# A state-space scan and an FP4 feed-forward on one core: D term as a matmul, ScalarE copies the sum out, TensorE's sums behind its other jobs

## The reference, cut to what matters

```python
x = silu(conv(x) + conv_b); xh = x.reshape(b, L, 4, 128)
dt_r, Bm, Cm = split(einsum('hod,blhd->blho', xw, xh))
delta = softplus(einsum('hdr,blhr->blhd', dtw, dt_r) + dt_b)
def step(s, inp):
    s = s * exp(d_t * A) + (d_t * u_t) * B_t
    y_t = einsum('bhdn,bhn->bhd', s, C_t)
...
y = ys + x * Dskip          # the D term
y = y * silu(z)
x = x + y @ out_proj_w.T
x = x + fp4_ffn(layernorm(x))
```

## Time and profile before

| | |
|---|---|
| median of three runs | 4897.47 us |
| the profiled execution | 4895.54 us |
| its span, first to last instruction | 4893.5 us |
| TensorE, matmul records / weight loads | 4234.6 us (87%) / 1986.9 us (41%) |
| VectorE | 4549.8 us (93%) |
| ScalarE | 3509.2 us (72%) |
| GpSimd | 3429.2 us (70%) |
| mean granted clock of TensorE | 0.988 of full speed |

### The profile page before, as it was taken

One profiled execution on the slowest core, in us unless ns is written; L12 is line 12 of the kernel. 1 busy time (PEld: TensorE's weight loads), 2 busy tenths in 40 slices (PEclk: granted clock), 3 DMA queues, 4 the chain that ended last, 5 costly groups with the idle time before them and its releaser, 6 DMA issues. The chain is left out here.

```text
span 4893.5 us, 64416 instructions
## 1 busy us (share of the span) xinstructions
PE 4234.6 (87%) x18927; PEld 1986.9 (41%) x19244; DVE 4549.8 (93%) x6828; ACT 3509.2 (72%) x5783; POOL 3429.2 (70%) x2321
## 2 busy tenths in 40 slices
PE   4788888888888888888898888888888888888887
PEld 1234444444444444444444444444444444444434
DVE  6999999999999999999999999999999999999994
ACT  3777777677777777777777777777777777777763
POOL 4777777777776777777777677777777677677763
PEclk8999999999999999999999999999999999999999
DMA  2333333333333333333333333333333333333330
GB/s 89 140 135 123 127 129 125 121 132 126 120 133 124 123 129 129 123 123 134 119 127 131 122 126 127 127 123 130 126 120 133 124 123 129 129 123 123 129 117 19
DMA packets 211138, 600.59 MB, mean 123 GB/s; under 512 B 25446, under 2 KB 76774, under 8 KB 210790
## 3 DMA queue, kind: packets, MB, share of 16 engines
q1 hardware_dynamic: 209088, 594.30, 35.6%
q10 hardware_dynamic: 1702, 2.16, 0.2%
HBM read 575.39 MB, written 20.97 MB: 122 GB/s over the span
## 5 line engine op out<-in xcount | busy, mean ns | idle before, releaser
L629 POOL TENSOR_TENSOR prod<-state,cs 128x1024 f32<-128x1024 f32 x1024 | 2416.5, 2360 | 1320.8 <-DVE state L852 1295.2
L440 ACT ACTIVATE decay<-delta,aneg 128x512 f32<-128x512 f32 x2048 | 1432.6, 717 | 925.3 <-DVE state L852 916.7
L840 DVE TENSOR_TENSOR db<-db,du 128x512 f32<-128x512 f32 x2048 | 1392.0, 680 | 56.7 <-PE db L904 55.5
L852 DVE TENSOR_TENSOR_SCAN state<-decay,carry,db 128x512 f32<-128x512 f32 x1024 | 1292.4, 1262 | 0.0
L852 DVE TENSOR_TENSOR_SCAN state<-decay,db 128x512 f32<-128x512 f32 x1024 | 1232.6, 1204 | 0.0
L904 PE MATMUL db<-pieces,sel 128*128 128x512 bf16 x1798 | 690.1, 386 | 393.5 <-DVE state L852 384.6
L919 PE MATMUL ybank<-prod,ident 64*64 64x512 f32 x4096 | 1003.4, 608 | 28.0 <-DVE hh L790 27.0
L919 PE MATMUL cross<-prod,ident 64*64 64x512 f32 x4096 | 1003.1, 609 | 0.0
L904 PEld LDWEIGHTS db<-pieces,sel 128*128 128x128 bf16 x2048 | 197.8, 97 | 1039.9 <-DVE state L852 809.0
L919 PEld LDWEIGHTS ybank<-prod,ident 64*64 64x64 f32 x4096 | 255.8, 134 | 455.1 <-issue 417.8
L1040 PE MATMUL bank_a<-wd,ht 128*128 128x256 f32 x1536 | 406.0, 389 | 3.2 <-DVE state L852 2.0
(11 more groups left out here) (124 smaller groups left out, 6399.6 us busy)
## 6 DMA issues: line engine op xcount, KB each, us to landing
cs<-c_rows SPq DMA_DIRECT2D x1024, 512.0 KB, 3.6
xin<-in_hidden SPq DMA_DIRECT2D x128, 128.0 KB, 3.6
xres<-in_hidden SPq DMA_DIRECT2D x128, 128.0 KB, 3.4
out_x<-ot SPq DMA_DIRECT2D x128, 128.0 KB, 3.6
c_rows<-xdbl SPq DMA_DIRECT2D x128, 32.0 KB, 3.6
win<-in_win_t SPq DMA_DIRECT2D x1, 1024.0 KB, 10.6
state<-in_w_gate ACTq DMA_DIRECT2D x1, 704.0 KB
state<-in_w_up ACTq DMA_DIRECT2D x1, 704.0 KB
```

The source lines that it names most:

```text
L440: act.activation(decay[:, g.val() % RING, :], delta[:, gu % 2, :], ACT.Exp, scale=aneg[:, gu % HEADS, gn:gn + 1]).then_inc(decayed, 1)
L629: pool.tensor_tensor(prod[:, r, :, :], state[:, 2 * p:2 * p + 2, :], cs[:, c, :, :], ALU.mult).then_inc(weighted, 1)
L840: dve.tensor_tensor(t[:, :], t[:, :], du[:, gu % 2, :], ALU.mult).then_inc(db_done, 1)
L852: dve.tensor_tensor_scan(state[:, n, :], decay[:, g.val() % RING, :], db[DB_BANK[g.k % TRIP]][:, :], start, ALU.mult, ALU.add).then_inc(sc ...
```

## The change

The D term is no longer computed by VectorE. Four diagonal matrices `ddiag` (one for each head, `dsk` on the diagonal) are built once at the start. TensorE multiplies them with `uu` directly behind the join, into the same bank, so `joined` tells that the sum is complete. ScalarE, in its slot 6, between the three decays and the second absolute value, copies the bank to `yg` and raises `y_taken`. Apart from that, TensorE's `step` calls `side` before the sums, in every slot. `alog` is placed into memory that `vt` uses later. After the edits line numbers behind each of them are a few higher.

```diff
@@ -155,10 +155,10 @@
         cw = sb("cw", [HEADS, TAPS])
         cb = sb("cb", [HEADS])
         cdiag = sb("cdiag", [HEADS, TAPS, P])
+        ddiag = sb("ddiag", [HEADS, P])
         xws = sb("xws", [HEADS, P])
         dtws = sb("dtws", [HEADS, P])
         dtb = sb("dtb", [HEADS])
-        alog = sb("alog", [HEADS, NST])
         aneg = sb("aneg", [HEADS, NST])
         dsk = sb("dsk", [HEADS])
         wo = sb("wo", [HEADS, DM])
@@ -201,6 +201,7 @@
         v2 = sb("v2", [DM])
         vs = sb("vs", [3, DM // BLK])
         vt = sb("vt", [KM, P])
+        alog = vt[:, 0, 0:HEADS * NST].rearrange("p (h n) -> p h n", h=HEADS)
         hh = sb("hh", [2, PADI])
         hv = [hh[:, i, 0:INNER] for i in range(2)]
         hs = sb("hs", [3, INNER // BLK])
@@ -461,6 +462,10 @@
                             wait(act, scanned, w.val(NST, (half + 1) * HALF_ST))
                             act.activation(carry[:, w.mod(HEADS), rows], state[:, rows, CH - 1],
                                            ACT.Copy).then_inc(carried, 1)
+                if w := due("scan", 22):
+                    wait(act, joined, w.val(plus=1))
+                    wait(act, op_mm, w.div(4, 4, -3))
+                    act.activation(yg[:, w.mod(8) // 4, w.mod(4), :], ybank[:, :], ACT.Copy).then_inc(y_taken, 1)
                 if t := due("norm", 13):
                     wait(act, st1, t.val(2, 2))
                     wait(act, xn_tp, t.val())
@@ -582,7 +587,7 @@
                     act.wait_ge(ld_const, CONSTS)
                     act.activation(aneg[:, :, :], alog[:, :, :], ACT.Exp).then_inc(a_exp, 1)
                 if j == -3:
-                    act.wait_ge(a_ready, 4 + HEADS * TAPS)
+                    act.wait_ge(a_ready, 4 + HEADS + HEADS * TAPS)
                 if w == W_DOWN:
                     act.wait_ge(zeroed, 1)
                     for k in range(KI):
@@ -742,11 +747,6 @@
                     dve.bn_stats(stats2[:, :], x1[:, t.mod(4), :]).then_inc(st2, 1)
                 if t := due("post", 18):
                     dve.bn_aggr(mv2[:, :], stats2[:, :]).then_inc(st2, 1)
-                if w := due("scan", 22):
-                    wait(dve, joined, w.val(plus=1))
-                    wait(dve, op_mm, w.div(4, 4, -3))
-                    dve.scalar_tensor_tensor(yg[:, w.mod(8) // 4, w.mod(4), :], uu[:, w.mod(4), :], dsk[:, w.mod(HEADS):w.mod(HEADS) + 1],
-                                             ybank[:, :], ALU.mult, ALU.add).then_inc(y_taken, 1)
                 if t := due("post", 36):
                     gated(t, 0)
                 if t := due("post", 38):
@@ -869,6 +869,9 @@
                     dve.tensor_copy(swap[:, 0:Q], ident[:, Q:P]).then_inc(a_ready, 1)
                     dve.tensor_copy(swap[:, Q:P], ident[:, 0:Q]).then_inc(a_ready, 1)
                     for h in range(HEADS):
+                        dve.tensor_scalar(ddiag[:, h, :], ident[:, :], dsk[:, h:h + 1], None,
+                                          ALU.mult).then_inc(a_ready, 1)
+                    for h in range(HEADS):
                         for k in range(TAPS):
                             dve.tensor_scalar(cdiag[:, h, k, :], ident[:, :], cw[:, h, k:k + 1], None,
                                               ALU.mult).then_inc(a_ready, 1)
@@ -890,10 +893,10 @@
                 gu, gn = g.k // NST, g.k % NST
                 if g.within(STEPS):
                     spread_b(b, g)
+                side(b, u, due)
                 for slot, pairs in SUMS.items():
                     if w := due("scan", slot):
                         sum_up(w, pairs)
-                side(b, u, due)
 
             def spread_b(b, g):
 
@@ -956,7 +959,8 @@
                     in_proj(v, 1, 1).then_inc(z_mm, 1)
                 if w := due("scan", 21):
                     wait(pe, cross_taken, w.val(plus=1))
-                    pe.matmul(ybank[:, :], swap[:, :], ycross, start=False, stop=True,
+                    pe.matmul(ybank[:, :], swap[:, :], ycross, start=False, stop=False, skip_group_check=True)
+                    pe.matmul(ybank[:, :], ddiag[:, w.mod(HEADS), :], uu[:, w.mod(4), :], start=False, stop=True,
                               skip_group_check=True).then_inc(joined, 1)
                 if v := due("pre", 16):
                     wait(pe, xd_evac, v.val(2, 2))
@@ -1078,7 +1082,7 @@
                 w = PLACE_AFTER.get(j)
                 if j == -4:
                     pe.wait_ge(ld_const, CONSTS)
-                    pe.wait_ge(a_ready, 4 + HEADS * TAPS)
+                    pe.wait_ge(a_ready, 4 + HEADS + HEADS * TAPS)
                 if w is None:
                     return
                 raw = w_raw[w]
```

## The result

The changed kernel takes 5004.47 us (median of four runs, 5002.53 to 5007.60); the kernel before took 4898.52 beside it. The ratio is 1.0216, 95% interval 1.0199 to 1.0234: slower by 2.2%, 106 us. Forecast were 4998 us, in a range of 4930 to 5050. The profiled execution took 5004.16 us; its span is 5002.1 us, 108.6 us longer than before.

What follows compares the result with a forecast made beforehand. VectorE bounds most slots, with detours over TensorE and ScalarE in slots 3 to 7 and 0 to 2. Profiled 4895.5 us plus 105 for 15 trips, -4 first eight units, +1 constants: 4998 us; range 4930 to 5050.

Steps and rivals of the forecast that it cites:

- the sum: Delays of slots 3 to 7 and 0 to 2 added over a trip's eight units: 6.99 us; 15 trips, 105 us.
- Place A, VectorE's relief: Slots 3 to 7: VectorE could reach its second gating 1.45 us earlier; 1.35 waited away on TensorE.
- Place A, ScalarE: Slots 3 to 7: copy ahead of second absolute value makes slot 7's rounding 0.38 us later, 0.32 without carry.
- Place B: Slots 0 to 2: TensorE waits for `xdbl` before the sums; slot 2's product 0.45 us later, 0.82 without carry.
- VectorE's relief counts: Rival: second up half and absolute value come in time; faster, 4811 or 4721 us; chance 0.13.
- A alone: Rival: slots 3 to 7 cost, slot 1's `db` matmul has slack enough; 4935 us; chance 0.09.
- B alone: Rival: slots 0 to 2 cost, ScalarE makes up 0.48 us before the rounding; 4960 us; chance 0.09.
- TensorE as the bound of slots 4 to 7: Rival: the D matmul's 0.86 us is not covered and pushes the second gating; 5060 us; chance 0.05.

Runs made afterwards that it cites:

- The fastest kernel: Changed kernel with slot-0 sums first, join and D matmul behind second up half, second absolute value after first decay, `yg` copy directly behind; 4727.79 us, ratio 0.9662.
- the kernel with the copy late: Changed kernel with slot-0 sums first, join and D matmul behind second up half, second absolute value after first decay, `yg` copy behind the decays; 4758.38 us.

## Why the prediction was right

- **The time.** 4998 was forecast and 5004.47 measured; +102 against the profiled execution, whose counterpart came out at +108.6. By parts of the trace: the 14 full trips from unit 8 to 119 grew from 295.2 to 302.8 us on average, 7.6 a trip where the sum had 6.99. The cause was right as well: both delays lie where the sum put them, and each goes with one edit.
- **Place A, VectorE's relief.** The first gating waits 0.68 us for the silu, the second 1.18 for the up half; forecast were about 0.6 and 1.3. The relief of 0.66 us a unit was indeed waited away, and the run without the D matmul shows that TensorE is not even what ends place A.
- **Place A, ScalarE.** The copy takes 0.48 us of ScalarE (1771.45 to 1771.93), the figure of the earlier rows; the 0.52 that comes out of the Trainium skill's formula ("ScalarE: Activation LUTs", What ACT_TABLE_LOAD costs), an estimate, does not fit it. The delay is 0.38 us in the carry unit of the timeline, as worked out; on average it is 0.40 with carry and 0.34 without, where 0.38 and 0.32 were forecast. The rounding's own wait is 0.50 to 0.56 us, not 0.4. The run with the copy behind the absolute value gives 0.49 us a unit back. That is the copy's whole step; A was put at less, 2.5 us a trip, because the 0.1 us that the second gate half gains was set off against it, and stays when the copy goes.
- **Place B.** TensorE started the `less` matmul 0.06 behind `xdbl`, and the `db` matmul 2.53 us later (1792.39 to 1794.92), to the hundredth the sum's figure. The product came 0.50 us later against 0.45: it starts 0.52 behind its matmul, not 0.49. On average B costs 0.50 us with carry and 0.83 without, where 0.45 and 0.82 were forecast. With the sums first in slot 0 the trip is 4.1 us shorter, not 4.5: in its first unit 0.43 us of what place B gives back come again in place A (14.04 to 14.47), which then starts late again as it did before the change.
- **What the sum mis-sized,** all small, and in part against each other. The 14 full trips grew by 105.9 us where the sum had 97.9, the last trip and the tail by 6.4 (4.0 in units 120 to 126, 2.4 from there to the end) where it had 7.0. The first eight units gained 5.5 us instead of 4, and the start cost 1.8 instead of 1. The largest part is the last unit of a trip: it had 0.38 and grew by 0.6 on average (38.77 to 39.36 us; single ones lie between 38.7 and 40.8 in the changed kernel). Place A is 0.40 us dearer there, as in the other carry units; the other 0.20 lie between the rounding and the product of slot 2 of the next unit (24.42 to 24.62), where the sum had nothing. They show with the D term's move alone (24.55) and with the sums first in slot 0 (24.73), and not with the reordering alone (24.42) or the copy behind the absolute value (24.45), so they come with the copy's place too; how, stays open.
- **Two signs that failed.** VectorE's busy time was to fall by about 90 us and its waiting to more than double. It fell by 60, and the time without work grew to 1.5 times (344 to 513 us), in one trip to 1.8 times (14.2 to 26.0). The D term's records are 94.5 us, but the other records became 10 us longer in sum, and a record overlaps the next one (by 0.08 us where 1725.82 + 1.24 ends behind 1726.98) only where no wait lies between. VectorE has some 270 more waits, which at 0.08 to 0.09 us are 22 to 24 us, an estimate. The delay of each unit was right even so, since it was worked out from starts.
- **The rivals.** VectorE's relief counts: false, both halves of the change alone are slower. A alone and B alone: false, each shows only in the run that holds one of the edits. TensorE as the bound of slots 4 to 7: false, by the run without its matmul. The Trainium skill's advice on offloading ("Perfetto Trace Analysis", Optimizing Scalar/DVE Operations), by which it may make sense where VectorE is saturated, did not hold for the change as made. The fastest kernel has VectorE free of the D term too and takes 4727.79 us, 3.4% less than before, but its queues are reordered besides, and that order with the D term left on VectorE was not run: what the offload itself is worth is not shown.

## What to carry to other kernels

Work taken off the fullest engine counts only if every detour that ends on that engine ends early enough; find for each the last instruction in front of the wait, and ask what the edit puts ahead of it in its queue. Here 0.48 us ahead of a small absolute value and one semaphore wait moved ahead of 1.9 us of matmuls turned VectorE's relief into a loss of 2.2%, and putting the urgent instruction first in three queues (TensorE, ScalarE, and by ScalarE's copy GpSimd) turned that into a gain of 3.4% with the same work. The longest wait in the list gave nothing when it was shortened in the changed kernel, because the rounding's wait stood behind it. With the copy out of the way it was the wait that ended place A, and without it and with an earlier absolute value the time fell by 120 us.

## What the runs showed that was not expected

The list of waits counts idle time from the end of the record before, so a real wait of 0.14 us a unit did not stand in it; only the distances between starts show such a wait. VectorE's block scaling (128x44) had a median of 191 ns and a longest of 327 in the kernel with the copy late, and 160 and 188 with it early; why it is slower when it follows a late maximum was not tried. And a move on ScalarE alone made VectorE wait for GpSimd, 7 us behind the copy that had come late (from 1714.33, where GpSimd's product by silu(z) could start, to 1721.39).
